# One attention-and-mixture pair after another: the order of a pair's jobs written anew on four engines

## The reference

```
Q, K, V = 16 heads of 16 columns of xn @ WQ, WK, WV
causal  = softmax(Q K^T / 4 + causal mask) V, heads joined, @ WO

q, k = rope(xn @ Wq), rope(xn @ Wk)            # 16 heads of 64
gate = the 2 best of 8 experts by sigmoid(xn @ Wsel), else 0
v    = sum over e of gate_v[e] * (xn @ Wv[h, e])
o    = softmax(q k^T / 8) v                    # no mask
src2 = sum over h, e of (gate_o[e] * o) @ Wo[h, e]
ffn  = layernorm(s + relu(s @ W1 + b1) @ W2 + b2),  s = layernorm(xn + src2)
```

## Time and profile before

| | |
|---|---|
| median of 3 runs | 3456.52 us (3451.72 to 3457.24) |
| the profiled execution's own time | 3454.12 us |
| its span | 3452.3 us |
| stretch before 219.5 us of the span, TensorE busy | 118.96 us |
| 219.5 to 3177.9 us (pairs), TensorE busy | 2864.18 of 2958.40 us |
| same stretch, VectorE, ScalarE, GpSimd busy | 2256.05, 1642.26, 1563.05 us |
| 3177.9 to 3452.3 us, TensorE busy | 260.98 of 274.40 us |
| TensorE's granted clock in the stretch of the pairs | 1.00 (of 2.4 GHz) |
| DMA share there | 0.33 |

### The profile page before, as it was taken

How to read it: one execution, slowest core, us unless ns; L and a number is a source line. 1 busy time by engine, 2 the same in 40 slices (tenths; PEclk the granted TensorE clock), 3 DMA queues, 4 the chain that set the end, 5 groups by cost and what they waited for, 6 DMA issues and landing times.

```text
span 3452.3 us, 64265 instructions
## 1 busy us (share of the span) xinstructions
PE 3244.1 (94%) x18240; PEld 2393.1 (69%) x18240; DVE 2541.3 (74%) x4708; ACT 1776.5 (51%) x3869; POOL 1706.5 (49%) x1855
## 2 busy tenths in 40 slices
PE   1699999999999999999999999999999999997998
PEld 1577777777777777777777777777777777774765
DVE  6577777777777777777777778777777777775554
ACT  2355555555555555555555555555555555553121
POOL 4254455556544565446644554545545654442122
PEclk9999999999999999999999999999999999999999
DMA  5233333234323333233233332333232433223121
GB/s 165 66 77 86 97 83 85 68 83 109 82 74 80 87 98 80 76 90 95 74 86 80 90 95 67 83 102 92 71 84 68 112 80 80 77 74 109 66 87 61
DMA packets 115937, 295.18 MB, mean 86 GB/s; under 512 B 33856, under 2 KB 54592, under 8 KB 99264
## 3 DMA queue, kind: packets, MB, share of 16 engines
q1 hardware_dynamic: 115904, 294.78, 31.9%
HBM read 262.74 MB, written 31.98 MB: 85 GB/s over the span
## 4 chain that ended last, share of the span: by engine, by line
PE 70%; DVE 23%; issue 4%; ACT 1%; DVEq 1%; POOL 1%; DMA 0%; SPq 0%; POOLq 0%; ACTq 0%
PE bank L690 21%; PE bank L816 13%; PE bank L735 8%; DVE uf L1223 7%; PE bank L790 7%; PE bank L705 5%; PE bank L922 4%; PE bank L914 3%; DVE nmax L1120 3%; DVE vm L1141 2%; PE bank L762 2%; PE bank L802 2%; PE bank L771 2%; DVE vm L1184 2%; PE bank L710 2%
## 5 line engine op out<-in xcount | busy, mean ns | idle before, releaser
L580 POOL TENSOR_TENSOR u_l<-uf,u_h 128x512 fp32r<-128x512 f32 x512 | 660.8, 1296 | 773.3 <-ACT u_h L1025 773.2
L690 PE MATMUL bank<-wv_h,xx 128*128 128x512 f32 x2048 | 749.8, 407 | 77.7 <-DVE vm L1141 77.7
L1120 DVE TENSOR_REDUCE nmax<-bank 128x1 f32<-128x512 f32 (+3 forms) x1024 | 553.2, 581 | 337.9 <-PE bank L705 323.1
L974 ACT ACTIVATE probs<-bank,nmax 128x512 f32<-128x512 f32 (+3 forms) x1024 | 591.3, 609 | 347.7 <-DVE nmax L1120 346.8
L690 PEld LDWEIGHTS bank<-wv_h,xx 128*128 128x128 f32 x2048 | 386.6, 189 | 234.7 <-DVE vm L1141 123.6
L1025 ACT ACTIVATE u_h<-uf 128x512 fp32r<-128x512 f32 x512 | 321.5, 628 | 381.7 <-DVE uf L1223 376.7
L1223 DVE TENSOR_TENSOR uf<-oo,go 128x512 f32<-128x512 f32 x512 | 504.8, 996 | 11.7 <-POOL u_l L580 9.5
L735 PE MATMUL bank<-ident_sb,probs 128*128 128x128 f32 x3328 | 454.4, 275 | 1.0 <-ACT stackT L1016 1.0
L735 PEld LDWEIGHTS bank<-ident_sb,probs 128*128 128x128 f32 x3328 | 386.3, 141 | 65.8 <-issue 14.3
L816 PE MATMUL bank<-u_h,wo_h 128*128 128x512 f32 x1024 | 421.5, 412 | 10.6 <-ACT u_h L1025 7.6
L816 PE MATMUL bank<-u_h,wo_l 128*128 128x512 f32 x1024 | 405.7, 396 | 0.0
(11 more groups left out here) (141 smaller groups left out, 5164.2 us busy)
## 6 DMA issues: line engine op xcount, KB each, us to landing
go<-go_d SPq DMA_DIRECT2D x256, 512.0 KB, 6.5
xx<-xs_d SPq DMA_DIRECT2D x128, 512.0 KB, 3.3
oo<-scale_d SPq DMA_DIRECT2D x128, 128.0 KB, 2.8
a_d<-a_out SPq DMA_DIRECT2D x128, 128.0 KB, 2.3
pt_c<-in_x SPq DMA_DIRECT2D x16, 512.0 KB, 4.5
st<-in_wv SPq DMA_DIRECT2D x16, 512.0 KB, 5.8
st<-in_wo SPq DMA_DIRECT2D x16, 512.0 KB, 7.5
go_d<-go_turned SPq DMA_DIRECT2D x256, 8.0 KB
```

Of the source, the lines that this page charges most:

```text
L580: nc.gpsimd.tensor_tensor(u_l[:, e % 2], uf[:, e % 2], u_h.bitcast(f32)[:, e % 2], ALU.subtract).then_inc(ul_done, 1)
L690: last = nc.tensor.matmul(out, lhs, rhs, start=n == 1, stop=n == 3 * len(chunks))
L974: nc.scalar.activation(probs[:, s % 2, j, 0:w], sbank[j][:, 0:w], ACT.Exp, bias=nmax[:, 2 * s + j:2 * s + j + 1], **kw).then_inc(exp_done, 1)
L1120: nc.vector.tensor_reduce(nmax[:, 2 * s + j:2 * s + j + 1], sbank[j][:, 0:w], AX.X, ALU.max, negate=True).then_inc(nmax_ready, 1)
```

## The change

The four tables are written anew, and RP becomes two jobs: RP 0 makes two of the four rope products, RP 1 the other two. The number of instructions of each kind is the same. Per body:

- TensorE: P 0 to P 3 stand together at the front of slot 0, with AT behind them. AC and V 0 fill slot 1. J 0 goes from slot 1 to 2, J 2 from 2 to 3, V 1 from 3 to 2. In slot 7, V 7 goes ahead of ST 0, ST 1 and J 7.
- ScalarE: in slot 0, all four copies of P, EX, UH 0 and UH 1; AC alone in slot 1; UH 2 in slot 2.
- VectorE: CH 0 from slot 1 to the front of slot 0, ahead of ON; CH 1 from slot 2 to 1. V 0 to V 2 each one slot earlier. YA after V 7.
- GpSimd: UL 0 and UL 1 in slot 1 with VA behind them; RP 0 and RP 1 on either side of UL 3; RS, PA, PB and VN later.

```diff
-PE_FILL = [[("AT", 0), ("P", 0), ("P", 1)],
-           [("P", 2), ("P", 3), ("J", 0), ("AC", 0)],
-           [("J", 1), ("V", 0), ("J", 2)],
-           [("V", 1), ("J", 3), ("V", 2)],
+PE_FILL = [[("P", 0), ("P", 1), ("P", 2), ("P", 3), ("AT", 0)],
+           [("AC", 0), ("V", 0)],
+           [("J", 0), ("V", 1), ("J", 1)],
+           [("V", 2), ("J", 2), ("J", 3)],
...
-           [("ST", 0), ("ST", 1), ("J", 7), ("V", 7)]]
+           [("V", 7), ("ST", 0), ("ST", 1), ("J", 7)]]
-ACT_FILL = [[("P", 0), ("UH", 0), ("P", 1), ("UH", 1)],
-            [("P", 2), ("P", 3), ("EX", 0), ("AC", 0), ("UH", 2)],
-            [("UH", 3)],
+ACT_FILL = [[("P", 0), ("P", 1), ("P", 2), ("P", 3), ("EX", 0), ("UH", 0), ("UH", 1)],
+            [("AC", 0)],
+            [("UH", 2), ("UH", 3)],
...
-DVE_FILL = [[("ON", 0), ("U", 0), ("U", 1)],
-            [("U", 2), ("CH", 0)],
-            [("U", 3), ("CH", 1)],
-            [("U", 4), ("V", 0), ("U", 5), ("V", 1)],
-            [("V", 2), ("U", 6), ("V", 3)],
+DVE_FILL = [[("CH", 0), ("ON", 0), ("U", 0), ("U", 1)],
+            [("CH", 1)],
+            [("U", 2), ("V", 0), ("U", 3)],
+            [("V", 1), ("U", 4), ("V", 2), ("U", 5)],
+            [("V", 3), ("U", 6)],
...
-POOL_FILL = [[("VC", 0), ("UL", 0)],
-             [("UL", 1)],
+POOL_FILL = [[("VC", 0)],
+             [("UL", 0), ("UL", 1), ("VA", 0)],
              [("UL", 2), ("RP", 0), ("UL", 3)],
-             [("VA", 0), ("RS", 0), ("UL", 4), ("PA", 0)],
-             [("UL", 5), ("PB", 0), ("VN", 0)],
-             [("UL", 6), ("SQ", 0)],
+             [("RP", 1), ("UL", 4), ("RS", 0)],
+             [("UL", 5), ("PA", 0), ("PB", 0)],
+             [("VN", 0), ("UL", 6), ("SQ", 0)],
...
                     elif name == "RP":
-                        proj_done()
+                        if e == 0:
+                            proj_done()
...
-                        nc.gpsimd.tensor_tensor(rot[:, 0], a, cos, ALU.mult)
-                        nc.gpsimd.tensor_tensor(rot[:, 1], c, sin, ALU.mult)
-                        nc.gpsimd.tensor_tensor(rot[:, 2], a, sin, ALU.mult)
-                        nc.gpsimd.tensor_tensor(rot[:, 3], c, cos, ALU.mult).then_inc(pool_step, 1)
+                        if e == 0:
+                            nc.gpsimd.tensor_tensor(rot[:, 0], a, cos, ALU.mult)
+                            nc.gpsimd.tensor_tensor(rot[:, 1], c, sin, ALU.mult)
+                        else:
+                            nc.gpsimd.tensor_tensor(rot[:, 2], a, sin, ALU.mult)
+                            nc.gpsimd.tensor_tensor(rot[:, 3], c, cos, ALU.mult).then_inc(pool_step, 1)
```

More of the change, by code:

```diff
@@ L53 @@
             [("SO", 0), ("SO", 1)]]
-DVE_FILL = [[("ON", 0), ("U", 0), ("U", 1)],
-            [("U", 2), ("CH", 0)],
-            [("U", 3), ("CH", 1)],
-            [("U", 4), ("V", 0), ("U", 5), ("V", 1)],
-            [("V", 2), ("U", 6), ("V", 3)],
+DVE_FILL = [[("CH", 0), ("ON", 0), ("U", 0), ("U", 1)],
[3 more added lines that the diff above has]
+            [("V", 3), ("U", 6)],
             [("V", 4), ("QL", 0), ("QL", 1), ("U", 7)],
             [("V", 5), ("RECIP", 0)],
-            [("V", 6), ("YA", 0), ("V", 7)]]
-POOL_FILL = [[("VC", 0), ("UL", 0)],
-             [("UL", 1)],
+            [("V", 6), ("V", 7), ("YA", 0)]]
+POOL_FILL = [[("VC", 0)],
+             [("UL", 0), ("UL", 1), ("VA", 0)],
              [("UL", 2), ("RP", 0), ("UL", 3)],
-             [("VA", 0), ("RS", 0), ("UL", 4), ("PA", 0)],
-             [("UL", 5), ("PB", 0), ("VN", 0)],
-             [("UL", 6), ("SQ", 0)],
+             [("RP", 1), ("UL", 4), ("RS", 0)],
+             [("UL", 5), ("PA", 0), ("PB", 0)],
+             [("VN", 0), ("UL", 6), ("SQ", 0)],
              [("SK", 0), ("UL", 7)],
```

## The result

| | before | after |
|---|---|---|
| median of 4 runs each | 3456.18 us (3451.72 to 3457.24) | 3417.80 us (3414.75 to 3420.71) |
| ratio, 95% interval | | 0.9891 (0.9874 to 0.9908) |
| the profiled execution | 3454.12 us | 3414.75 us |

The forecast was 3420 us, within 2.2 us of the median. That alone proves little: two terms could be wrong and cancel. So I go through the profile in the order in which the prediction did.

What follows compares the result with a forecast made beforehand. TensorE, busy 94% of the span, bounds the kernel. Waits removed, 1.43 us, less new ones of 0.75 and 0.1, give 0.58 us a body, x 62 = 36 us: 3420 us as a median, 8 in 10 within 3373 to 3464.

Steps and rivals of the forecast that it cites:

- waits of V 2 and V 3 removed: On TensorE, the waits before V 2 and V 3 for VectorE's gates both go: 1.43 us a body gained.
- V 0's gate over, V 2 comes: From AT's end, VectorE frees V 0's bank at 10.3 us and TensorE reaches V 2 at about 12: no wait.
- new wait at the scores of slot 3: TensorE waits for ScalarE's exponentials of slot 2, behind UH 1: 0.75 us a body added, bounds 0 to 1.3.
- wait at J 3, with the slower restart: TensorE waits at J 3 for UL 3, now behind UL 2 and two rope products on GpSimd: 0.1 us added.
- QK 1: On TensorE, QK 1 starts 0.38 us after J 5; the 0.14 us lost a body stays unchanged.
- late loads of `xx`: Second half of `xx`, loaded behind V 7 and needed by P 2: covered, 1 us in all if the longest falls there.
- first and last bodies: Prologue, first and last body have few jobs of both kinds: costed at nothing.
- changes of shape: TensorE's switches of matmul shape are as many as before: 0 within 0.1 us a body either way.
- The meeting of U and UL: VectorE's U 3 waits out GpSimd's UL 2, then takes some 0.55 us; the next GpSimd instruction is later by 0.4.
- The slower rival: VectorE's U 3 and U 4 lose their turn to successive GpSimd instructions: +0.57 us a body, 3492 us; chance 0.14.
- The covers costed at nothing: Copies of four projections in a row (0.35 us spare) and CH 0 ahead of ON (0.4 us spare) cost nothing.
- The rival "better": No new wait at the scores of slot 3, U 0 and U 1 being quicker: 89 us gained, 3368 us; chance 0.17.

## Why the prediction was right

Step by step, with the forecast first:

| term | forecast | measured |
|---|---|---|
| waits of V 2 and V 3 removed | 1.43 us | 1.45 us |
| V 0's gate over, V 2 comes (from AT's end) | 10.3, 12 us | 10.5, 12.1 us |
| V 1's gate over, V 3 comes | 14.0, 17 us | 14.3, 17.5 us |
| new wait at the scores of slot 3 | 0.75 us | 0.60 us |
| wait at J 3, with the slower restart | 0.1 us | 0.30 us |
| QK 1 | 0.14 us, stays | 0.14 us |
| usual body | 46.70 us | 46.67 us |
| mean body | 46.70 us | 46.80 us |
| late loads of `xx`, over all bodies | at most 1 us | some 7 us |
| first and last bodies | nothing | 10 us shorter |

**The sum.** 1.45 - 0.60 - 0.30 = 0.55 us of the 0.61 by which the usual body got shorter. The 0.06 that is left lies within the 0.1 left open for changes of shape, and I can't place it. So the mechanism is as forecast, at the places named. In the body two errors nearly cancel: the wait at the scores was taken 0.15 too long, and J 3's 0.2 too short. The first because TensorE's own work up to the scores takes 4.99 us (1018.08 to 1022.71, and 0.36 for turn 1) and not 4.81 (V 0 was counted at 1.45 where its row gives 1.48; turn 1, turn 0 and V 0 are each a little longer in the new order); the chain on ScalarE was right to 0.1 us. The second because the prediction had UL 3's end right (14.9 us from AT's end, measured 15.0) but set it directly against J 3's turn. The hand-over of 0.15 us and the slower first step behind a wait were left out.

**Luck in the time.** That the time came out within 2 us is not owed to this sum alone. Over the pairs the late loads of `xx` took back some 7 us of the forecast gain, and the first and last bodies gave 10 that it didn't have. Two terms that the prediction put at next to nothing stood against each other. Behind AT of the last body, TensorE's timeline before has marked waits of 2.00, 1.04 and 1.29 us at J; after the change the longest there is one of 1.01 us, at the scores. No run takes the ends apart further.

**The meeting of U and UL.** It goes as the rows of before have it: U 3 ends 0.54 us after UL 2, where some 0.55 was forecast, and the product behind UL 2 takes 1.19 us. The slower rival, in which VectorE loses its turn to a row of GpSimd instructions, does not occur: U 3 gets in after one. The Trainium skill ("SBUF — State Buffer", "Who interferes with whom") says that a VectorE instruction with two SBUF inputs contends with a GpSimd one that reads SBUF, and that whoever is first blocks the other whole. By that, the trace agrees; and also in what it exempts, as the gate with one input from a bank takes its 0.69 us (1033.59) while a rope product runs.

**The covers costed at nothing.** ScalarE's copies of P stand 0.9 to 1.07 us apart, and no P or AT waits for one:

```profile
1011.57 0.49 ACT L1006 ACTIVATE raw<-bank 128x384 f32<-128x384 f32 x1 [0.31 <-PE bank L693]
1012.49 0.49 ACT L1006 ACTIVATE raw<-bank 128x384 f32<-128x384 f32 x1 [0.42 <-PE bank L693]
```

CH 0 does not hold ON up. UL 4 ends at 1036.75 and J 4 comes at 1037.06 without a wait, with the 0.3 us to spare that the forecast called nothing.

**Where a step was too easy.** The load of `xx` was costed with the landing times of before, and these have moved: the median from 3.3 to 4.0 us, the longest from 6.6 to 7.1. Where a load lands late P 2 now waits for it, as it is needed earlier in the body.

**What carried the gain.** The prediction counted waits and asked no more. The experiments add what each part is for: the early gate is the gain, and CH 0 beside AT (2.3 us), the split of the rope (1.9 us) and V 7's place (0.2 us, by its time) are what keeps the new order from paying for it elsewhere. And they show what it didn't need: two swapped pairs of entries in the old order give the same time. TensorE's new list was not tried by itself, so what it contributes alone is not shown. The rival "better" failed where the prediction said, at UH 1 in a list in which nothing can pass it; with that one entry moved, the time is 3359 us, under its 3368.

## What to carry to other kernels

In hand-ordered lists, put a read-out that frees a bank ahead of work that nobody waits for yet, and never put an instruction that waits for another engine ahead of one that is already due and that the busiest engine needs (UH 1 ahead of the exponentials cost 0.9 us a body). Measure the busiest engine's losses from start to start, walk each removed wait forward to what is late next, and try the one-entry swap before the new order. Where GpSimd and VectorE run side by side, count each VectorE product with both inputs in SBUF at its own time plus what is left of the GpSimd instruction under way, as the rows of these traces have it. And count the first and last bodies too: they held a quarter of this gain.

## What was not expected of the hardware

- **A wait may cost more than its length.** In two runs TensorE waited for 2.0 and 2.4 us in each body, and behind this the granted clock fell to a mean of 0.70 and 0.64 over 4 us in 27 and 25 of the 62 bodies, which then took 1.6 and 1.2 us more. Waits of 1.3 us or less left it alone. Why some bodies are hit and others with the same wait aren't stays open.
- **One small VectorE product took 1.39 us instead of 0.29,** because a GpSimd instruction of 1.3 us had just begun. Reductions and the reciprocal of the same size beside GpSimd kept their times (0.28 and 0.95 us, the reciprocal in the kernel before and in the run with the split alone).
- **The first matmul behind even a short wait** takes 0.32 us to the next start instead of 0.23, as at J 3, where the wait is 0.2 us.
